# Causal attention on one core: products with the values in three blocks a stage instead of six

## What is computed

```python
c_q = x @ W_dq
Q = (c_q @ W_uq).reshape(B, S, 16, 8)
c_kv = x @ W_dkv
K = (c_kv @ W_uk).reshape(B, S, 16, 8)
V = (c_kv @ W_uv).reshape(B, S, 16, 8)
scores = einsum('bqhd,bkhd->bhqk', Q, K) / sqrt(8)
scores = where(causal, scores, -inf)
attn = softmax(scores, axis=-1)
out = einsum('bhqk,bkhd->bqhd', attn, V).reshape(B, S, 128)
return out @ W_o
```

## Time and profile before

| what | value |
|---|---|
| median of 3 runs | 1451.42 us (1448.87 to 1455.66) |
| profiled execution, its own time | 1451.36 us |
| its span | 1449.6 us |
| PE busy | 1268.6 us |
| DVE busy | 1129.5 us |
| ACT busy | 930.0 us |
| attention stages, scores to last product | about 84 to 566 us |

### The profile page before, as it was taken

One profiled execution on the slowest core, in us unless ns is written; L12 is line 12 of the kernel. 1 busy time (PEld: TensorE's weight loads), 2 busy tenths in 40 slices (PEclk: granted clock), 3 DMA queues, 4 the chain that ended last, 5 costly groups with the idle time before them and its releaser, 6 DMA issues. The chain is left out here.

```text
span 1449.6 us, 30335 instructions
## 1 busy us (share of the span) xinstructions
PE 1268.6 (88%) x10501; PEld 718.9 (50%) x10501; DVE 1129.5 (78%) x2980; ACT 930.0 (64%) x2597; POOL 705.3 (49%) x742
## 2 busy tenths in 40 slices
PE   4689999999999997369999999699599999996991
PEld 2323333333343333336666666565366666665551
DVE  5788888888888861669899998566599989995667
ACT  4437777776777674748888887232488888883320
POOL 1011222122212221469999999110599999992102
PEclk9859999999999998579999999799899999998896
DMA  4431111111112002001211111000012111110001
GB/s 112 134 104 50 56 42 38 40 59 44 38 38 60 14 5 84 18 23 31 51 31 31 31 33 36 1 1 1 15 33 55 31 31 31 31 31 9 1 1 58
DMA packets 35055, 55.45 MB, mean 38 GB/s; under 512 B 6978, under 2 KB 22732, under 8 KB 32588
## 3 DMA queue, kind: packets, MB, share of 16 engines
q1 hardware_dynamic: 34328, 53.37, 14.0%
q10 hardware_dynamic: 576, 0.15, 0.1%
HBM read 26.77 MB, written 8.39 MB: 24 GB/s over the span
## 5 line engine op out<-in xcount | busy, mean ns | idle before, releaser
L516 ACT ACTIVATE a_prob<-a_psE 128x512 f32<-128x512 f32 (+3 forms) x768 | 318.3, 500 | 140.5 <-PE a_psE L444 137.9
L444 PE MATMUL a_psE<-a_qs,a_ks 84*128 84x512 bf16 (+3 forms) x768 | 248.3, 336 | 17.4 <-ACT a_prob L516 8.3
L599 DVE CUSTOM_DVE_ANT_0 a_psM<-a_psM,mask_q 128x384 f32<-128x384 f32 (+3 forms) x512 | 242.4, 507 | 18.6 <-PE a_psM L432 18.0
L432 PE MATMUL a_psM<-a_ks,a_qs 72*128 72x512 bf16 (+3 forms) x768 | 250.3, 343 | 5.7 <-PEq L86 3.2
L1089 POOL TENSOR_TENSOR w_rn<-w_ssm,mhalf 128x16 f32<-128x16 f32 x64 | 213.6, 3337 | 66.7 <-DVE w_ssm L1129 66.7
L551 POOL TENSOR_SCALAR_AFFINE_SELECT a_prob<-a_prob 128x512 f32<-128x512 f32 x128 | 81.1, 634 | 332.5 <-ACT a_prob L516 307.9
L601 DVE TENSOR_REDUCE a_nm<-a_psM 128x1 f32<-128x512 f32 x256 | 175.8, 687 | 46.6 <-PE a_psM L432 46.6
L1031 ACT ACTIVATE w_prob<-w_psS,w_bias 128x128 f32<-128x128 f32 x512 | 179.8, 376 | 21.4 <-DVE w_bias L1155 21.2
L1079 POOL TENSOR_TENSOR w_t<-w_raw,w_sin 128x256 f32<-128x256 f32 x256 | 178.6, 729 | 0.0
L444 PEld LDWEIGHTS a_psE<-a_qs,a_ks 84*128 84x128 bf16 x768 | 74.5, 98 | 180.3 <-ACT a_prob L516 97.1
L1084 POOL TENSOR_TENSOR w_rot<-w_t 128x1024 f32<-128x1024 f32 x64 | 150.9, 2358 | 8.8 <-issue 0.4
(11 more groups left out here) (136 smaller groups left out, 2371.5 us busy)
## 6 DMA issues: line engine op xcount, KB each, us to landing
w_vb<-w_v SPq DMA_DIRECT2D x128, 128.0 KB, 2.3
a_qs<-q_parts SPq DMA_DIRECT2D x16, 576.0 KB
a_ks<-k_parts SPq DMA_DIRECT2D x16, 576.0 KB
q_parts<-p_parts SPq DMA_DIRECT2D x24, 128.0 KB
k_parts<-p_parts SPq DMA_DIRECT2D x24, 128.0 KB
out_x<-l_y SPq DMA_DIRECT2D x8, 256.0 KB, 2.3
a_qs<-a_nmT SPq DMA_DIRECT2D x32, 48.0 KB
w_wqkv<-in_wqkv SPq DMA_DIRECT2D x2, 768.0 KB, 7.4
```

What stands on the lines that cost most here:

```text
L432: pe.matmul(out, qs[0:ROWS, g, j, i * P:(i + 1) * P], ks[0:ROWS, g, j, 512 * kc:512 * kc + n], start=True, stop=True).then_inc(m_ready, 1)
L444: pe.matmul(psE[:, r % NRING, 0:w], ks[0:KROWS, g, j, kt * P:(kt + 1) * P], qs[0:KROWS, g, j, q0:q0 + w], start=True, stop=True).then_inc( ...
L516: act.activation(prob[G % NPROB][:, j, 0:w], psE[:, r % NRING, 0:w], ACT.Exp, scale=SCALE0).then_inc(e_read, 1)
L599: dve.tensor_tensor_reduce(scores, scores, sb["mask_q"][:, 512 - n:512], -1.0, -3.0 * NEG, ALU.add, ALU.min, low).then_inc(m_read, 1)
```

## The change

The constant for the lag goes, and the products of four groups are issued together, after the scores of groups 4, 8 and 0. The last four groups follow after the loop.

```diff
-AV_LAG = 2
+AV_GROUPS = 4
...
-                if G % 2:
-                    for behind in (AV_LAG + 1, AV_LAG):
-                        if G >= behind:
-                            values(G - behind)
-            for G in GROUPS[-AV_LAG:]:
+                if G % AV_GROUPS == 0 and G > 0:
+                    for behind in range(AV_GROUPS, 0, -1):
+                        values(G - behind)
+            for G in GROUPS[-AV_GROUPS:]:
                 values(G)
             turn_outputs(NSTAGE - 1, 1)
```

## The result

The changed kernel takes 1538.45 us (median of 4, 1536.96 to 1540.99) against 1453.24 us (4 runs of before): a ratio of 1.059, 95% interval 1.057 to 1.062, so 85 us slower. The prediction had the sign, but 1505 us, and the time lies just above its range (1538).

What follows compares the result with a forecast made beforehand. It took PE, DVE and ACT, all within some 15% of the stage period and joined by short rings, as the bound. 1451.4 + 30 (rings less PE's saving) + 24 (clock) = 1505 us, range 1470 to 1538.

Steps and rivals of the forecast that it cites:

- the sign: Whole kernel: slower, with chance 0.89, against 0.06 for faster and 0.05 for the same.
- Saved on PE: Blocks of products with the values: three instead of six a stage save PE 0.5 to 0.8 us a stage.
- Lost at the rings: PSUM buffers to ACT and DVE, empty after each block: fewer blocks hide less work, costing 2.6 us a stage.
- The walk: Step through one attention stage in the new order using traced durations: 31.2 us against 29.16, so +2.1 us.
- each entry: Gap before a block's first product: about 0.1 us, three a stage.
- The clock: PE's granted clock in the steady attention stages: one short fall a stage, 1.7 us each, 24 us in all.
- the nearer row: First clock fall inside attention, 3.4 us at the low level, taken as the length of each fall.
- (a): Rival for the attention stages: the rings drain but the clock holds, 1481 us; chance 0.30.
- (d): Rival for the whole kernel: savings and new waits cancel within 0.5%, 1444 to 1459 us; chance 0.05.
- (b): Rival for the attention stages: clock falls more than once a stage and stays low longer, 1529 us and more; chance 0.15.
- (c): Rival for the attention stages: PE is the bound and its partners have slack, 1439 to 1443 us; chance 0.06.

Runs made afterwards that it cites:

- the last filled run: Changed kernel with sixteen added f32 products a stage, none before the first maxima unit behind a block: 1505.1 us, ratio 1.038.
- The cut of DVE's reads: DVE reads only 128 columns of every maxima unit, in both kernels: 1451.9 us for the kernel before, 1449.5 us for the changed kernel.
- the run of the first part: Kernel before with only the products of groups 4 to 7 merged into one block, after the scores of group 8: 1476.4 us, ratio 1.016.
- its control: Kernel before with only the copies of the outputs put ahead of the exponentials of groups 6 and 2: 1444.9 us, ratio 0.9944.

## Why the prediction was right and wrong

*Saved on PE: right, and small.* Blocks of 2.29, 2.35 and 3.57 us against 2.27, 2.27 and 3.55. The sum saved is 0.4 us a stage, just under the lower end of what I gave (0.5 to 0.8).

*Lost at the rings: right to 0.2 us a stretch.* The walk had 7.65, 8.9 and 6.3 us and 0.1 for each entry, so 7.75, 9.0 and 6.4; the runs show 7.79 (the last filled run, clock held), 8.79 and 6.43. The errors cancel, and the stage is 31.2 us as forecast, 2.1 more than before, 29 us over 14.25 stages. The idle times behind the block of groups 4 to 7 came near what I gave, too: 3.61 us for ACT (3.5) and 2.81 for DVE (3). The cut of DVE's reads shows the cause. What ACT's pace in groups 5 to 8 costs was not measured by itself; with the cut, it and the saving on PE about cancel.

*The clock: right mechanism, mis-sized term.* This is the step that failed. I took one spell of 3.4 us at the low level a stage, worth 1.7 us: 24 us in all. The fourteen stages have a mean clock of 0.87, which is 0.13 x 489 / 0.5 / 14 = 9.1 us at the low level a stage, and they last 34.98 - 31.2 = 3.8 us longer than the sum of the pieces at full clock: 54 us in all. So I had a third of the low time and less than half of its cost. In groups 1 to 4 the clock fell in 14 stages of 14, in groups 9 to 0 in 7 of 14, and 17 of these 21 spells lasted about 6.8 us, like the second of the earlier trace rows, not like the first. Groups 1 to 4 grew from 7.79 to 9.04 us on average, the block behind them from 2.29 to 3.37, groups 9 to 0 from 6.43 to 7.21 and their block from 2.34 to 2.99: 3.8 us together. I chose the nearer row for the length, and had no reason from the rows for one spell a stage and not two. Each of the 21 spells ended inside a block of products with the values, and in the new order these are up to 9 us away. But a block does not always bring the level back: the spell of 20.5 us in the run of the first part went through three. Why most spells were the long kind stays open.

*The sum.* 29 + 54 = 83 us of the measured 85. The first and last stages, which I did not split, can hold the rest.

*Rivals.* (a), the clock holds: excluded by the granted clock itself. (d), savings and waits cancel: excluded by the time. (b), more than one fall and longer spells, with 0.15, is what happened; its 1529 "and more" should have carried more weight and the range should have reached past it. (c), PE alone bounds: excluded, since in the changed kernel a cut on DVE alone takes the loss away. The demand of the Trainium skill (TensorE: Matmul & The Clock Gate, Why this matters for your kernels) for no long idle gaps was too weak a test here: in groups 1 to 4 PE's weight loads waited for DVE 0.6 us at most each time [the waits above], and the level fell in every stage.

## What to carry to other kernels

Ask of a block of work on one engine how long it is against what the rings to its partners hold, partner by partner. Here blocks of two groups were the best of the three sizes: one group was 12.5 us slower than its control, and four groups left DVE so far behind that it set PE's pace. And once a partner sets PE's pace, look at the granted clock as well as at the waits. Here no single wait of PE for DVE was over 0.8 us, and the low level cost nearly twice what the waits did (54 and 29 us).

## What the runs showed of the hardware

More work made the kernel faster. Sixteen useless f32 products a stage, 3.4 us of PE's stream, kept the granted clock at 1.00 in the steady stages and took 34 us off the time (1538.45 to 1504.4). And the stretches of groups 5 to 8 kept the full level in all 14 stages, with 8.79 us between two blocks of products with the values, while groups 1 to 4, a shorter stretch that DVE paces (7.79 us at full clock), lost it in every stage. What PE streams in them, estimated from the columns of the rows at 2.4 GHz and 0.45 us for the transposes of the outputs, is 7.1 us in the first and 5.1 us in the second.

The level also stayed low where PE was hardly ever idle. In the run of the first part it did so for 20.5 us (PE busy for 20.3), with three blocks of products with the values in it and a stretch of 6.7 us (6.71 busy). The trace of the kernel before has the same at the start of the attention, where PE has scores and twice the maxima scores to do. Windows, columns as in the earlier trace rows:

```profile
84.00:88.00 4.00, 4.00 (x12) 1.52 (x10) 3.60 (x10) 2.27 (x4) 0.00 (x0) 0.50 0.69 155
88.00:92.00 4.00, 4.00 (x12) 1.67 (x11) 4.00 (x10) 1.56 (x4) 0.00 (x0) 0.50 0.46 123
...
100.00:104.00 4.00, 3.72 (x21) 1.18 (x14) 1.54 (x7) 0.96 (x2) 1.44 (x5) 0.66 0.28 51
```

It rose at 103 us, during the first block of products with the values (99.6 to 103.2). So neither a PE without gaps nor such a block was enough by itself. Whether f32 products on all 128 rows count otherwise for the clock than bf16 scores on 72 and 84 rows was not tried; the added products were of the first kind alone.
